# Attention with routed experts: the side jobs of a quad moved between its steps, and SyncE's transfers of a quad put in another order

## The reference

```python
qkv = x @ w_qkv + b_qkv                                  # heads of 8, split in q, k, v
attn = softmax(einsum('bhqd,bhkd->bhqk', q, k) * scale)
vals = einsum('bhqk,bhkd->bhqd', attn, v)                # back to (B, S, 128)
x = layernorm(x + vals @ w_out + b_out)
gates = sigmoid(x @ Wg); vals, idx = top_k(gates, 2); vals = vals / vals.sum(-1)
shared = silu(x @ Ws1) * (x @ Ws3) @ Ws2
h = silu(einsum('td,edf->tef', x, We1)) * einsum('td,edf->tef', x, We3)
routed = einsum('tef,efd,te->td', h, We2, w)             # w: the two gate values
out = layernorm(x + (shared + routed) / 3)
```

## Time and profile before

| | |
|---|---|
| median of 3 runs | 690.12 us (687.95 to 690.82) |
| the profiled execution | 686.2 us, of which 684.5 us span |
| busy | PE 640.4, DVE 548.9, ACT 424.2, POOL 269.4 us |
| mean granted TensorE clock | 0.980 |
| ramp, until the first exponential | about 37 us |
| stages 0 to 32 | about 37 to 503 us |
| experts | about 503 to 684.5 us |

### The profile page before, as it was taken

One profiled execution on the slowest core, in us unless ns is written; L12 is line 12 of the kernel. 1 busy time (PEld: TensorE's weight loads), 2 busy tenths in 40 slices (PEclk: granted clock), 3 DMA queues, 4 the chain that ended last, 5 costly groups with the idle time before them and its releaser, 6 DMA issues.

```text
span 684.5 us, 16202 instructions
## 1 busy us (share of the span) xinstructions
PE 640.4 (94%) x4653; PEld 320.8 (47%) x4653; DVE 548.9 (80%) x1272; ACT 424.2 (62%) x973; POOL 269.4 (39%) x402
## 2 busy tenths in 40 slices
PE   8899999999999999999999999999899989999970
PEld 5442333333334333333343334333258878888760
DVE  4895677779897997998899799797667767888882
ACT  2065677776676776677767667766734346666752
POOL 3322112333144335314434432540525526677772
PEclk9998899999999999999999999999999999999995
DMA  4557466344433324442333342330132033444522
GB/s 84 122 122 175 100 137 156 82 88 105 74 84 79 84 50 78 96 89 62 85 72 64 89 101 53 66 89 15 52 108 63 32 83 88 146 141 132 164 74 77
DMA packets 161857, 62.68 MB, mean 92 GB/s; under 512 B 110586, under 2 KB 155516, under 8 KB 161808
## 3 DMA queue, kind: packets, MB, share of 16 engines
q1 hardware_dynamic: 155008, 46.72, 31.2%
q0 software_dynamic: 5648, 13.26, 6.4%
q10 hardware_dynamic: 1152, 2.10, 0.8%
HBM read 38.04 MB, written 24.26 MB: 91 GB/s over the span
## 4 chain that ended last, share of the span: by engine, by line
PE 64%; issue 11%; POOL 8%; DVE 7%; DMA 4%; ACT 4%; SPq 2%; POOLq 0%; ACTq 0%; DVEq 0%
PE pvp L1051 16%; PE scoreB L1026 15%; PE scoreA L1012 14%; POOL y_dram L1242 6%; DVE mx L946 4%; DMA parts_dram<-parts 3%; ACT prob L919 2%; PE shared L534 2%; PE scoreB L1527 2%; PE shared L523 2%; PE pvp L995 1%; PE shared L518 1%; PE shared L553 1%; POOL prob L1227 1%; PE shared L542 1%
## 5 line engine op out<-in xcount | busy, mean ns | idle before, releaser
L919 ACT ACTIVATE prob<-scoreB 128x512 f32<-128x512 f32 x512 | 278.7, 600 | 125.9 <-PE scoreB L1026 125.5
L946 DVE TENSOR_REDUCE mx<-scoreA 128x2 f32<-128x1024 f32 x256 | 304.5, 1219 | 65.1 <-PE scoreA L1012 62.5
L1026 PE MATMUL scoreB<-qs,ks 74*128 74x512 bf16 x512 | 197.0, 387 | 6.4 <-ACT prob L919 3.0
L1012 PE MATMUL scoreA<-ks,qs 72*128 72x512 bf16 x512 | 195.2, 386 | 4.7 <-DMA ks<-parts_dram 2.4
L1051 PE MATMUL pvp<-prob,v 128*32 128x512 f32 x1024 | 137.6, 611 | 0.8 <-ACT pv_sb L911 0.8
L1012 PEld LDWEIGHTS scoreA<-ks,qs 72*128 72x128 bf16 x512 | 49.6, 99 | 138.9 <-DVE mx L946 65.1
L1026 PEld LDWEIGHTS scoreB<-qs,ks 74*128 74x128 bf16 x512 | 49.3, 97 | 100.3 <-ACT prob L919 77.6
L1242 POOL DMA_INDIRECT y_dram<-prob x72 | 70.8, 983 | 44.2 <-issue 30.7
L497 POOL DMA_INDIRECT slots_dram<-rows,slot_i x64 | 63.3, 990 | 56.5 <-DMA ks<-parts_dram 31.4
L846 POOL CAST parts<-qk 128x256 bf16<-128x256 f32 x32 | 12.7, 396 | 180.9 <-ACT v_raw L572 169.6
L1601 PE MATMUL scoreB<-w,prob 128*128 x288 | 44.2, 276 | 1.1 <-DVE prob L1414 1.1
(11 more groups left out here) (178 smaller groups left out, 921.0 us busy)
## 6 DMA issues: line engine op xcount, KB each, us to landing
qs<-parts_dram SPq DMA_DIRECT2D x96, 96.0 KB
parts_dram<-parts SPq DMA_DIRECT2D x32, 192.0 KB
slots_dram<-blank POOLq DMA_DIRECT2D x9, 520.0 KB, 7.2
prob<-slots_dram SPq DMA_DIRECT2D x72, 65.0 KB, 1.9
ks<-parts_dram SPq DMA_DIRECT2D x64, 64.0 KB
prob<-y_dram SPq DMA_DIRECT2D x8, 512.0 KB, 3.3
ks<-parts_dram SPq DMA_DIRECT2D x32, 96.0 KB
xin<-in_L_attn_x SPq DMA_DIRECT2D x32, 64.0 KB, 2.2
```

What stands on the lines that cost most here:

```text
L919: act.activation(prob[:, i % 2, j, 2 * u + c, :], scoreB[:, c], ACT.Exp, scale=SCALE).then_inc(exp_done, 1)
L946: dve.tensor_reduce(mx[:, i % 2, at // 2, at % 2 * 2:at % 2 * 2 + 2], scoreA[:, at % 2], AX.X, ALU.max).then_inc(max_done, 1)
L1012: ins = pe.matmul(scoreA[:, at % 2, c], qs[0:KR, st, j, qc * P:(qc + 1) * P], ks[0:KR, st, j, :], start=True, stop=True)
L1026: pe.matmul(scoreB[:, c], ks[0:KM, i, j, kc * P:(kc + 1) * P], qs[0:KM, i, j, :], start=True, stop=True).then_inc(b_ready, 1)
```

## The change

In a quad, x is turned at step 2 (before 4), projected at step 4 (before 6), and the values are turned at step 6 (before 3), or at step 5 where i is 1. `counts` goes from step 2 to 3, and the three pieces of `place` in quad 1 from steps 3, 5, 7 to 4, 6, 7. The two early tiles of the ramp follow (`SOONER`). SP loads the stack first in a stage; the parts of tile q+4 are then stored in the stage that makes them, after the maxima, the next x tile (one quad sooner) and the weights, and not in the stage after. On POOL, `deviation` moves from the start of a stage to behind `v`. The loop runs four batches and not five; the fifth is written out.

```diff
-    SOONER = [("xT", 2, -3, 7), ("qkv", 2, -3, 7), ("xT", 3, -2, 4), ("qkv", 3, -2, 6)]
+    SOONER = [("xT", 2, -3, 7), ("qkv", 2, -3, 7), ("xT", 3, -2, 2), ("qkv", 3, -2, 4)]
...
-        if at == 2 and i == 1 and (inner or 2 <= b <= self.batches):
+        if at == 2 and not early and (inner or s + 4 < self.quads):
+            kinds.append("xT")
+        if at == 3 and i == 1 and (inner or 2 <= b <= self.batches):
             kinds.append("counts")
-        if at == 3 and (inner or 0 <= s - 2 < self.quads):
+        if at == 4 and not early and (inner or s + 4 < self.quads or 0 <= s + 1 < self.quads):
+            kinds.append("qkv")
+        if at == (5 if i == 1 else 6) and (inner or 0 <= s - 2 < self.quads):
             kinds.append("valsT")
-        if at == 4 and not early and (inner or s + 4 < self.quads):
-            kinds.append("xT")
...
-            with eng.Fori(2, B - 1) as b:
+            with eng.Fori(2, B - 2) as b:
...
-            for s in range(QUADS - 4, QUADS + 1):
+            for s in range(QUADS - 8, QUADS + 1):
...
+            def store_parts(b, i):
+
+                q, par = 4 * b + i, i % 2
+                need(sp, split_done, q + 5)
+
+                need(sp, stack_loaded[par], 16 * STACK_DMAS * (2 * b + i // 2 + 2))
+                sp.dma_start(parts_dram[par].rearrange("k h i p t -> p (k h i) t"),
+                             parts[:].rearrange("p k h i t -> p (k h i) t")).then_inc(parts_stored, 16)
...
                 if has(b, i, 3):
-
-                    n, par = q + 3, (i + 3) % 2
-                    need(sp, split_done, n + 1)
...
+                    load_stack(b, i)
+                if ramp:
+                    store_parts(b, i)
+                if has(b, i, 1):
+                    load_maxima(b, i)
+                if has(b, i, 5) and not (isinstance(b, int) and q < -1):
+                    load_x(b + (i + 1) // 4, (i + 1) % 4)
+                if isinstance(b, int) and 0 <= q < 8:
+                    load_expert_weights(q)
...
+                if has(b, i, 4) and not ramp:
+                    store_parts(b, i)
                 if routing(b) and i == 0:
                     store_x1(sp, b - 1)
...
-                    if i == 1 and at == 2 and routing(b):
+                    if i == 1 and at == 3 and routing(b):
                         read_counts_job(dve, b)
-                    if i == 1 and at >= 3 and at % 2 and routing(b):
-                        place(dve, b - 2, at // 2 - 1)
+                    if i == 1 and at in PLACES and routing(b):
+                        place(dve, b - 2, PLACES.index(at))
```

More of the change, by code:

```diff
@@ L739, in load_expert_weights, with load_stack @@
                     sp.dma_start(w2[:, E], ws2.rearrange("(c f) d -> f c d", f=P)).then_inc(experts_loaded, 16)
+            def load_stack(b, i):
+                q, par, st = 4 * b + i, (i + 3) % 2, (i + 3) % 4
+                need(sp, parts_stored, 16 * (q + 4))
+                if has(b, i, -1):
+                    need(sp, b_ready, 16 * q)
+                if isinstance(b, int) and q + 3 < 4:
+                    sp.wait_ge(ones_set, q + 4)
+                for r in range(3):
+                    sp.dma_start(qs[PR * r:PR * (r + 1), st],
+                                 parts_dram[par, 0].rearrange("h i (d c) t -> (i d) h (c t)", d=HD)) \
+                      .then_inc(stack_loaded[par], 16)
+                for row, i0, i1 in K_ROWS:
+                    sp.dma_start(ks[row:row + HD * (i1 - i0), st],
+                                 parts_dram[par, 1, :, i0:i1].rearrange("h i (d c) t -> (i d) h (c t)", d=HD)) \
+                      .then_inc(stack_loaded[par], 16)
@@ new lines, in load_maxima @@
+            def load_maxima(b, i):
+                sp.wait_ge(job_read, jobs.number("mT", b, i) + 1)
+                for m in range(2):
+                    sp.dma_start(qs[KR + m:KR + m + 1, (i + 1) % 4].rearrange("p h x -> p (h x)"), m2[:, m, :]) \
+                      .then_inc(m_loaded, 16)
+            def store_parts(b, i):
[4 more added lines that the diff above has]
+                             parts[:].rearrange("p k h i t -> p (k h i) t")).then_inc(parts_stored, 16)
@@ L741, in stage @@
             def stage(b, i):
                 q = 4 * b + i
[L743 removed]
+                ramp = isinstance(b, int) and q < 0
+                if isinstance(b, int) and q == -4:
                     load_x(-1, 2)
                     load_x(-1, 3)
[L746 to L747 removed]
                 if has(b, i, 3):
[L750 to L755 removed]
@@ L756, in load_maxima @@
[L756 to L766, removed]
-                    need(sp, parts_stored, 16 * (n + 1))
-                    if has(b, i, -1):
-                        need(sp, b_ready, 16 * q)
-                    st = (i + 3) % 4
-                    if isinstance(b, int) and n < 4:
-                        sp.wait_ge(ones_set, n + 1)
-                    for r in range(3):
-                        sp.dma_start(qs[PR * r:PR * (r + 1), st],
-                                     parts_dram[par, 0].rearrange("h i (d c) t -> (i d) h (c t)", d=HD)) \
-                          .then_inc(stack_loaded[par], 16)
-                    for row, i0, i1 in K_ROWS:
-                        sp.dma_start(ks[row:row + HD * (i1 - i0), st],
-                                     parts_dram[par, 1, :, i0:i1].rearrange("h i (d c) t -> (i d) h (c t)", d=HD)) \
-                          .then_inc(stack_loaded[par], 16)
@@ L783, in stage @@
-                if has(b, i, 1) and ramp:
-                    load_maxima()
+                    load_stack(b, i)
[7 more added lines that the diff above has]
+                    load_expert_weights(q)
                 if finishing(b) and i == 0:
@@ L832, in stage @@
                 q = 4 * b + i
-                if finishing(b) and i == 2:
-                    deviation(pool, b)
                 if scattering(b) and i == 3:
@@ L862, in stage @@
                                        bv[:, None].broadcast_to([P, 4, NCH, HD]), ALU.add).then_inc(v_ready, 1)
+                if finishing(b) and i == 2:
+                    deviation(pool, b)
                 if routing(b) and i == 0:
```

5 lines of the change are left out of this document (1 added, 4 removed).

## The result

The changed kernel takes **705.62 us** (median of 4 runs, 701.57 to 708.76) against 689.04 before: 1.025 times as long, with an interval of 1.020 to 1.030. Forecast were 687.4 us and a range to 695. The profiled execution has a span of 702.1 us, 17.6 more than before.

What follows compares the result with a forecast made beforehand. PE was taken to set the end, with 64% of the chain of waits. Fillers -0.6, routed batches +2.7, first stages -3.9 and tail -0.9 sum to -2.7 us: 687.4 us against a median of 690.1, range 682.5 to 695.0.

Steps and rivals of the forecast that it cites:

- SP and the first stages: Stages 1 and 2: 2.5 us of waits replace 6.4 of waits and slow clock, -3.9 us (-6.4 to +3.9).
- The price of a fall: Early stages: time lost when PE's clock drops to half after a wait, taken as 3.9 us each.
- the rival, the maxima behind the stack: Stages 1 and 2: both waits grow to 1.58 us, the clock falls after each, 695.2 us; chance 0.18.
- Landed 5.6 later: Stage 1: the stack of tile 4 starts from 54.0 and lands 5.6 us later at 59.6, in time for 60.6.
- the projection and the store are that much sooner: Stage 0: projection and store come two steps, 2.65 us, sooner, so the store goes out at 46.7.
- Routed batches: Loop batches with routing: side jobs wait for DVE, +0.5 us each (0 to +1.0), +2.7 in all (0 to +5.5).
- the starved DVE: Quad 2 of a routed batch: the projection between the scores of steps 4 and 5 starves DVE for 0.68 us.
- The new wait of x behind L607: Quad 3 of a routed batch: the turn of x needs DVE's read of the maxima, a new wait of 0.56 us.
- the lower end: Routed batches: three slow DVE instructions fall free of POOL's split, 1.3 us less DVE work, so a batch costs 0.
- Fillers: Quads without routing in the first two batches: jobs at even steps save 0.15 us a quad, -0.6 us (0 to -1.8).
- Tail: Quads 30 and 31: the turn of the values goes under PE's wait for ACT, 0.45 us each, -0.9 us.
- Counted at nothing: Loads that pass on SP, POOL's later `deviation`, the quad 3 scatter and the batch written out: 0 us.

Runs made afterwards that it cites:

- second execution: The changed kernel as it is, executed and profiled again: 698.34 us.
- old table: The changed kernel with the side jobs and the places of counts and place of the kernel before: 697.39 us.
- mended ramp: The changed kernel, but in the ramp's last stage SP loads quad 0's maxima ahead of the store of tile 3's parts: 693.53 us, 1.004 of the kernel before.
- maxima ahead: The mended ramp with the maxima loaded ahead of the stack in all later stages too: 692.37 us, 1.011 of the kernel before.
- new table alone: The kernel before with only the side jobs and the places of counts and place of the change: 690.99 us, 1.0035 of the kernel before.

## Why the prediction was wrong, step by step

*SP and the first stages (-3.9): wrong, +6.05.* The step that failed is that I read SP's new order in stages 1 and 2 and took stage 0 as it was. The ramp has an order of its own in the change (`if ramp: store_parts`), and there the store went ahead of the maxima of quad 0: a wait of 1.60 us that stands nowhere in the sum, with 24 us at half clock behind it. The price of a fall, 3.9, was that of one row; stage 0 alone lost 8.4. In stages 1 and 2 the old loss of 5.6 did go (14.07 and 13.39 for 15.76 and 17.09), but partly by luck: the slow start itself put the store of stage 0 far behind the 1 MB of weights. In the second execution, without the fall in stage 0, the loss came back in the manner of the rival, the maxima behind the stack, though not in its sizes: in stage 3, for the stack as well as for the maxima, with waits of 3.2 and 3.2 where I took 1.58 (ahead of stage 2 it was 0.54, for the stack), and with one fall and not two. "Landed 5.6 later" and "the projection and the store are that much sooner" were sums from one execution; from the store of stage 0 to its stack it can be 3.9 or some 8 us, perhaps by a race with POOL's clear, which I named only as a transfer that runs there.

*Routed batches (+0.5 each, bounds 0 to +1.0): mis-sized, +1.26 on average and +1.65 in the batch shown.* Of the mechanism, the starved DVE was right and came to 1.1 us in that batch (idle time of DVE: 59.88 - 52.17 = 7.7 against 6.6). Two things failed. The new wait of x behind L607 was put in quad 3 only (0.56; measured 0.43); quad 1 has it too, 0.58, most likely since the projection at step 4 of quad 0 starves DVE as that of quad 2 does. Quad 1 was given only 0.5 for a late `mT` of quad 2, which no row shows; it takes 0.85 more in that batch, and all of this goes when the projections of quads 0 and 2 go back. And the lower end took the contention with POOL as falling away; it moved and grew, by 0.5 of DVE time, as these rows of DVE's timeline show against the earlier trace rows:

```profile
322.88 0.51 DVE L467 CAST slot_i<-slot 128x8 int32<-128x8 f32 x1
...
351.50 0.54 DVE L364 TENSOR_TENSOR tmp<-g,top 128x32 f32<-128x32 f32 x1
...
355.80 0.60 DVE L378 TENSOR_TENSOR tot<-top 128x4 f32<-128x4 f32 x1
...
370.43 0.18 DVE L448 TENSOR_TENSOR tmp<-pos,room 128x32 f32<-128x32 f32 x1
```

L448 did fall free, as reckoned, and so did L473 (0.17 for 0.52), but L375 still takes 0.50, and L467, L364 and L378 are slow now (before 0.17, 0.19, 0.15). L467 and L364 run beside the split; L378 runs beside POOL's copies of `rows` (L486, 355.22 to 356.39), which the prediction did not look at. The rule that I cited (the Trainium skill, "GPSIMD Engine Reference", "1. Specifications") names DVE instructions in a 2-port mode beside those with two SBUF inputs; the cast L467 has one input, and no run here shows its mode. Not in the sum at all was that such waits, 0.27 and 0.58 close together, can be followed by a fall of the clock: 4.4 us once.

*Fillers (-0.6): right for a plain quad.* It takes 13.39 against 13.65, 0.26 less where I had 0.15; the pair with the values at an even step takes 3.28 (taken: 3.39). Over stages 4 to 8 that leaves -0.3, since the quad with i = 3 takes 15.40 for 15.17.

*Tail (-0.9): right.* From the turn of stage 30 to the pvp that waits for `pv_sb` are 23.74 us, before 24.58: 0.84 less, and PE waits for ACT at scoreB four times there and not six.

*Counted at nothing:* the loop's count and `deviation` cost next to nothing in a batch (58.32 with both and the old table, 58.23 before).

What the sum left out outweighs all of its terms. The mean granted clock was 0.960 after and 0.980 before: 0.040 x 702.1 = 28.1 us not granted, against 0.020 x 684.5 = 13.7, so that some 14 of the 17.6 us would be the clock's, if PE had been held up by nothing else while it was low. By the turns it is some 11, an estimate: 9.1 in stages 0 and 1 (against the profile of the mended ramp), 4.4 and 1.7, less the 3.9 of before.

## What to carry to other kernels

Read a new order of a queue in each stage that has its own branch, the ramp first, and look there for a small load that the first instruction of the main loop needs. A filler is free for the engine that waits, not for its neighbour: a long job put between two producers starves the engine that reads them, and if that one is nearly as full as PE (52.2 of 59.9 us), the time comes back as PE's waits. Judge a start by several executions: in three kernels that are the same up to stage 8, the load behind one store could start 3.9, 7.7 and 8.3 us after it. And compare variants by their ratio to one kernel that was measured beside each of them, not by their medians alone.

## What the runs showed of the hardware

- Short waits can cost far more than their length. After single idle times of 1.4 to 1.8 us in the first stages the clock did not fall at all (1.77, second execution of the changed kernel; 1.53, maxima ahead), or fell to 0.50 for some 3 us (1.40, new table alone), for 10 (1.58, before), for 24 (1.60, the changed kernel) or for 31 (1.63, old table). In the changed kernel PE was then busy for 10.00 of 10.00 us in two stretches at 0.50. The Trainium skill, "TensorE: Matmul & The Clock Gate", "What's actually happening", says that activity releases the throttle; here a busy PE had to go on at 1.2 GHz for 24 us.
- A store of 192 KB that goes out 0.33 us ahead of a clear of 520 KB on another engine's queue was followed by its dependent load after 3.9 to 5.4 us in six profiles and after 7.7 to 9.5 in five. The Trainium skill, "DMA: Bandwidth & Descriptors", "Queues, rings and completion order", has a DMA engine take turns between its queues. That the later clear holds up the store would fit this; the four profiles with the clear behind the store (4.7 to 5.2 us) agree with it and don't settle it.
- Two loads of 4 KB each were issued in 1.26 us right behind the loads of a stack (mended ramp), and in 4.34 us right behind a store of 192 KB on the same queue (changed kernel).
